# Eleven slots for gathered chunks in place of eight, and VectorE's wait for the stores of h put ahead of its first one-hot

## The reference

```python
x = x + gnn(layernorm(x), weight, src, dst, edge_weight)
#   h = einsum('nf,ef->ne', layernorm(x), weight)
#   gnn = segment_sum(edge_weight[:, None] * h[dst], src, 8192)
x = x + ffn(layernorm(x))
#   a few features of each row are read as digits, go through 7 layers of
#   width 160, and 2.0 is added at two one-hot places where a mask holds
```

## Time and profile before

| what | us |
|---|---|
| median of 3 runs | 1811.07 (1810.07 to 1818.78) |
| the profiled execution | 1809.53 |
| its span, first to last instruction | 1807.8 |
| PE busy | 1635.4 |
| DVE busy | 1178.1 |
| POOL busy | 1065.4 |
| ACT busy | 606.0 |

### The profile page before, as it was taken

The page is one execution under the profiler, slowest core; times in us unless marked ns, Lnnn a source line. Parts: engine busy times, 40 slices in busy tenths (PEclk is TensorE's granted clock), DMA queues, the critical chain, the costliest instruction groups (busy, mean ns, idle before and its releaser), DMA issues.

```text
span 1807.8 us, 29342 instructions
## 1 busy us (share of the span) xinstructions
PE 1635.4 (90%) x4076; PEld 651.0 (36%) x4077; DVE 1178.1 (65%) x4538; ACT 606.0 (34%) x1356; POOL 1065.4 (59%) x1114
## 2 busy tenths in 40 slices
PE   6699998799999999999999899999999999996895
PEld 3355553333333323333334233333333333332442
DVE  9366763587777788778777878787743333335455
ACT  6577742122222222222222222222234444443341
POOL 1000003677777777777767677777777777775930
PEclk9899999899999999999999999999999999998798
DMA  9311113677777776776667677676677777772334
GB/s 360 140 65 70 65 65 115 179 209 208 209 206 209 207 209 192 200 201 193 195 189 200 195 197 201 194 197 190 194 204 209 209 210 209 210 208 78 129 109 137
DMA packets 121766, 323.92 MB, mean 179 GB/s; under 512 B 20434, under 2 KB 39154, under 8 KB 121586
## 3 DMA queue, kind: packets, MB, share of 16 engines
q0 software_dynamic: 81920, 268.50, 52.6%
q1 hardware_dynamic: 39666, 53.48, 8.3%
HBM read 288.35 MB, written 33.55 MB: 178 GB/s over the span
## 4 chain that ended last, share of the span: by engine, by line
PE 59%; DVE 15%; issue 8%; DMA 6%; POOL 5%; DVEq 3%; SPq 3%; ACT 1%; ACTq 0%; POOLq 0%
PE psum L1174 39%; PE psum L1084 11%; POOL region L510 5%; DMA region<-h_rows,region 5%; DVE region L896 5%; PE psum L1253 4%; SPq L410 2%; DVEq L896 2%; DVE region L812 2%; DVE region L802 2%; PE psum L1073 1%; DVE region L814 1%; DVE region L806 1%; DVE region L816 1%; DVE region L808 1%
## 5 line engine op out<-in xcount | busy, mean ns | idle before, releaser
L510 POOL DMA_INDIRECT region<-h_rows,region x1024 | 985.2, 962 | 647.4 <-DMA h_rows<-region 289.0
L1174 PE MATMUL psum<-region 128*128 x2552 | 1236.8, 616 | 96.2 <-DVE region L896 49.5
L1174 PEld LDWEIGHTS psum<-region 128*128 128x128 f32 x2552 | 431.3, 189 | 863.5 <-issue 858.3
L896 DVE SCALAR_TENSOR_TENSOR region<-region 128x128 f32 (+1 forms) x1276 | 450.5, 353 | 439.0 <-PE psum L1174 299.4
L664 ACT ACTIVATE x<-psum 128x512 f32<-128x512 f32 x192 | 114.6, 597 | 792.5 <-PE psum L1174 792.5
L1084 PE MATMUL psum<-region 128*128 128x512 f32 x512 | 233.6, 600 | 15.8 <-ACT region L579 15.8
L816 DVE COPY_PREDICATED region<-region 128x128 f32<-128x128 int32 x452 | 158.6, 351 | 0.0
L812 DVE COPY_PREDICATED region<-region 128x128 f32<-128x128 int32 x452 | 158.0, 350 | 0.0
L647 ACT ACTIVATE psum<-x 128x512 f32<-128x512 f32 x256 | 153.7, 601 | 8.0
L802 DVE TENSOR_TENSOR region<-region 128x128 int32<-128x128 f32 x452 | 130.1, 288 | 25.0 <-ACT region L599 23.4
L814 DVE TENSOR_TENSOR region<-region 128x128 f32<-128x128 f32 x452 | 135.9, 301 | 0.0
(11 more groups left out here) (149 smaller groups left out, 642.2 us busy)
## 6 DMA issues: line engine op xcount, KB each, us to landing
x<-in_x SPq DMA_DIRECT2D x16, 1024.0 KB, 14.7
h_rows<-region SPq DMA_DIRECT2D x64, 256.0 KB, 2.0
region<-h_rows,region POOLq DMA_INDIRECT x1024, 3.7
out<-x SPq DMA_DIRECT2D x4, 2816.0 KB, 10.8
out<-x SPq DMA_DIRECT2D x8, 640.0 KB, 3.4
region<-in_L_gnn_weight SPq DMA_DIRECT2D x1, 1024.0 KB, 5.7
region<-in_src SPq DMA_DIRECT2D x4, 128.0 KB, 8.4
region<-in_dst SPq DMA_DIRECT2D x4, 128.0 KB, 8.1
```

The source lines that it names most:

```text
L510: pool.indirect_dma_start(gathered[:, (c + 1) % RING, :], None, h_dram, bass.IndirectOffsetOnAxis(ap=dst_i[g][:, i:i + 1], axis=0),).then_ ...
L896: dve.scalar_tensor_tensor(spread[:, slot % SR, :], iota_n[:, bass.ds((tile - (g * T + 1)) * P, P)], src_f[g][:, bass.ds(chunk - (g * NC + ...
L1174: pe.matmul(banks[:, bass.ds(pe.snap(tile_wanted) % AGG, 1), :].rearrange("p t f -> p (t f)"), spread[:, slot % SR, :], gathered[:, bass.d ...
```

## The change

RING goes from 8 to 11: `gathered`, the free semaphore's distance, the landing semaphores (`s_gat`, one a slot) and the modulo on TensorE follow it, and everything behind `gathered` in `region` moves by 3 x 512 words. VectorE's wait for the stores of h moves from its place after the ninth one-hot, ahead of the four clears, to the place ahead of the first one-hot and its register load.

```diff
-    RING = 8
+    RING = 11
@@
             dve.wait_ge(s_mm, T)
+            for u in range(4):
+                dve.wait_ge(s_hst[u], 16 * (T // 4))
             for g in range(PARTS):
                 following = second if g == 0 else sort_edges(g + 1)
                 for i, slots in enumerate(slots_with_steps(g)):
@@
                     if g == 0 and i == SR:
-                        for u in range(4):
-                            dve.wait_ge(s_hst[u], 16 * (T // 4))
                         for cleared in (all_fwT, all_fw_in, bias.rearrange("p h l -> p (h l)"), fw_out[:, :]):
                             dve.memset(cleared, 0.0).then_inc(s_fz, 1)
```

## The result

The changed kernel takes 1806.76 us (median of 20 runs, 1803.51 to 1814.54), the kernel before 1812.24 in as many runs on the same chip (1810.07 to 1820.68). The ratio is 0.9963, with a 95% interval of 0.9952 to 0.9975. The forecast was 1804.5 with a range of 1801.5 to 1810.0.

The account below looks back on a forecast made before the run. GpSimd's gathers were taken to bound the early and last stretches, VectorE's one-hots and sort the middle. Terms -3.8 - 3.8 + 0.4 + 0.6 = -6.6 took the median 1811.1 to 1804.5 us, range 1801.5 to 1810.0.

Parts of the forecast that it names:

- The end of part 2: After the last sort GpSimd sets the pace again and stands three chunks further ahead: -3.8 us, bounds -3.8 and 0.
- The lead at the weight loads: Three more gathers issue while SyncE starts the feed-forward loads; GpSimd's lead is taken up before part 1: -3.8 us.
- I take all of it: Counts GpSimd's whole 3.8 us lead from the weight loads as gained, though VectorE's room in part 0 may be less.
- the first rival: VectorE in part 0 has no room, so only the end of part 2 gains: -2.8 us, 1808.3; chance 0.20.
- 79% busy: Sign for no room in part 0: VectorE is as busy at 450 to 550 us as in the full parts.
- TensorE's 1.07 us a chunk: TensorE's floor against GpSimd's 1.255 us a chunk, giving 18 us of room over 100 chunks; 4.2 wanted.
- The wait: Wait for stores of h ahead of the first one-hot: VectorE's queue moves 2.8 us, costing +0.4, bounds 0 and +2.8.
- The swallowing: VectorE's 13.57 us wait for TensorE's transpose, after the feed-forward loads, absorbs the rest of its 2.8 us delay.
- The remainder by 11: TensorE's sequencer computes chunk modulo 11 for each step, nearer to two more operations: +0.6 us, 0 to +3.
- the dear remainder: Rival: modulo by 11 costs much more on TensorE's sequencer; slower from 0.24 us extra, 1819 at 0.5; chance 0.06.
- The middle: From 700 to 1300 us VectorE is full: slots gain 0, 447 or 448 gathers, some 35 us of real ring waits.
- that rival: The ring itself bounds the middle, so its 35 us of waits go too: 1769.5 us; chance 0.04.

Follow-up runs that it names:

- experiment 2: Changed kernel with RING back at 8, so only VectorE's wait moved; 1811.28 us, ratio 1.0008 to the kernel before.
- experiment 1: The changed kernel run and profiled once more, nothing altered; 1807.04 us, ratio 0.9986 to the kernel before.
- experiment 4: Changed kernel with eight slots and the 19 feed-forward weight loads issued one per chunk from chunk 16; 1803.81 us, ratio 0.9964 to the kernel before.
- experiment 11: Changed kernel, eleven slots, part 0's sort pieces ordering keys only, weights left in place (output not the reference's); 1803.13 us, ratio 0.9954 to the kernel before.
- experiment 12: Changed kernel with eight slots, part 0's sort pieces ordering keys only (output not the reference's); 1810.66 us, ratio 0.9994 to the kernel before.
- experiment 3: Changed kernel, eleven slots, the 19 feed-forward weight loads issued one per chunk from chunk 16; 1804.46 us, ratio 0.9955 to the kernel before.
- experiment 5: Changed kernel, eleven slots, weight copies of part 0's sort pieces shrunk to one word a partition; 2012.61 us where the kernel before takes 2015.75.
- experiment 10: Changed kernel with eight slots, weight copies of part 0's sort pieces shrunk to one word a partition; 2033.03 us, ratio 0.9991 to the kernel before.

## Why the forecast held, and where it was wrong

*The end of part 2: right.* -3.8 forecast; from chunk 768 to 800 the two executions win 3.9 each on the kernel before, 3.5 by the ring alone with the loads spread out. It is there after 32 chunks, where some 20 were forecast.

*The lead at the weight loads: wrong.* The step that failed is "I take all of it". The hole shrank as forecast (7.9 to 4.33 us), and the lead was there, but "From 350 to 630 us they follow GpSimd's pace without holding it up once" proved only that GpSimd never met the ring. It was taken as room on VectorE, and there was none: with the gathers 3.9 us ahead the one-hots came at most 0.2 earlier, and the term measured +0.2 and -0.6. The bound written beside it, "0, if VectorE has no room", is what happened, and the first rival named the mechanism with its place and its sign of 79% busy, at a chance of 0.20. That percentage was the better witness: VectorE is 79% busy where it is full, in the middle parts (235.55 of 300 us), so 79% in part 0 was a warning that it has next to no room there. The forecast trusted a wait's absence over it. The rate of TensorE's 1.07 us a chunk was no floor in this stretch, for the one-hots come slower when pieces of the sort lie between them.

*The wait: right in size, and gone by part 1.* +0.4 forecast at the weight loads, 0.3 measured there in experiment 2, and by chunk 288 it is gone. The swallowing was not complete: VectorE's later wait for the transpose fell from 13.57 to 11.68 us, so it took up 1.9 of the 2.8. The rest, 0.9 us in the changed kernel (0.4 to 0.7 in experiments 1 and 2), stays in the one-hots of part 0 until its last steps.

*The remainder by 11: nothing.* +0.6 forecast, 0.0 measured, in the register operations (93.9 ns on average in both kernels) and in the waits ahead of a turn. The lower bound held, and the dear remainder is out.

*The middle: right.* 446 gathers against a forecast of 447 or 448, and 33 us of real waits against 35. The ring was not a bound there, so that rival is out, and the rule of the Trainium skill that led to it (page "SBUF — State Buffer", section "Who interferes with whom") has next to no effect here: a gather beside the sort has a median of 947 ns, as in the earlier trace rows. The median hides a little: of the 447 gathers of the earlier trace rows, the 181 during which one of the sort's copies (L806) runs take 970 ns on average, the others 960.

*The sum.* -6.6 was forecast. The terms as measured add to about -4 (end -3.9, lead 0, wait 0.3 and gone, remainder 0), the aggregation shows -4.1 and -4.0, and the medians of 20 runs each differ by 5.5 (by 4.0, 1806.7 against 1810.7, if only the lower group of either is taken, as below experiment 4). That the difference came so near to the forecast is in part luck with the last stage: of 20 runs of the changed kernel one is above 1810, of the kernel before seven are above 1817. By mechanism the kernel is the first rival, 1808.3, and the measured 1806.76 is nearer to that (1.5) than to the 1804.5 of the forecast (2.3).

## What to carry to other kernels

More slots in a ring pay once for each place where the engine behind them turns from being held up to setting the pace, so many slots times its period, and nothing per chunk in between; they also bridge a still stand of the relay, but only if the engines after it have room to take the lead up. Look for that room in the consumer's own load, compared with a stretch where it is known to be full, not in the producer's waits: a producer that is behind never meets the ring, whatever the consumer has left. A batch of transfers issued inside a loop that relays semaphores holds up everyone behind the relay: 12.1 us of issuing cost 9 us at the next chunk here, and issuing one per turn won 7 to 8 us by the end of the aggregation, more than the three slots.

## What the runs showed of the hardware

The last stage has two lengths in one and the same program, 163.3 and 169.8 us in the two profiles of the changed kernel. Of the eight profiled executions on ordinary chips, five have 161 to 164 us and three 170 (the first of the changed kernel, and experiments 11 and 12); the three are in the upper group of their kernel's times and the five in the lower. The long ones have a lower granted clock near the end, as in the windows above, 0.70 against 1.00; which of the two brings about the other is not shown. Which length an execution gets moves its time by 6 to 7 us, more than the change does.

Chips differ far more than the change does: before takes 1811 to 1812 us on those of the result and of experiments 1 to 4, 11 and 12, and 2016 and 2033 on two others. There, in experiments 5 and 10, a gather still has a median of 946 to 949 ns and a matmul of 592, but single register operations take up to 1.4 us (1.1 in the rows shown). One run of experiment 4 took 2038.4 among eleven between 1801 and 1811 on an ordinary chip. I have no profile of that one, so whether it is the same thing is open.
